# Two conv-sweep layers on one core: token scaling by a table of turns, uneven reciprocal groups, and norm stores from ScalarE's queue

## What is computed

```python
def sweep_fwd(seq, w):
    def step(carry, row):
        new = row + jax.nn.relu(conv1d(carry, w))
        return (new, new)
...
x = x + _L0_conv_ref(_ln_c(x), L0_conv_w_d, ...)      # norm 0, then the sweeps
t = t + _L0_ffn_ref(_ln_t(t), ...)                    # norm 1, then the experts
x = x + _L1_conv_ref(_ln_c(x), L1_conv_w_d, ...)      # norm 2, then the sweeps
t = t + _L1_ffn_ref(_ln_t(t), L1_ffn_W, ...)          # norm 3, batch statistics, then the recurrence
...
def step(yt, wx_t):
    yt = jax.nn.sigmoid(wx_t + yt @ Vt)
```

## Time and profile before

| what | value |
|---|---|
| time, median of 3 runs | 4235.26 us (4232.78 to 4238.69) |
| the profiled execution's own time | 4230.19 us |
| its span, first to last instruction | 4228.4 us |
| mean granted TensorE clock | 0.99 |
| TensorE matmuls busy | 4126.6 us (98%) |
| ScalarE busy | 2062.3 us (49%) |
| VectorE busy | 1328.9 us (31%) |
| norms 0, 1, 2, 3 in the chain that ended last | about 3 to 93, 948 to 1243, 1257 to 1371, 2228 to 2399 us |

### The profile page before, as it was taken

One profiled execution on the slowest core, in us unless ns is written; L12 is line 12 of the kernel. 1 busy time (PEld: TensorE's weight loads), 2 busy tenths in 40 slices (PEclk: granted clock), 3 DMA queues, 4 the chain that ended last, 5 costly groups with the idle time before them and its releaser, 6 DMA issues.

```text
span 4228.4 us, 138285 instructions
## 1 busy us (share of the span) xinstructions
PE 4126.6 (98%) x57200; PEld 3129.7 (74%) x57200; DVE 1328.9 (31%) x2576; ACT 2062.3 (49%) x8972; POOL 119.9 (3%) x243
## 2 busy tenths in 40 slices
PE   8999999998889999999998899999999999999999
PEld 3999999994442999999993466666666666666666
DVE  4655433334546655533335600000000000000000
ACT  6002344435545002344444366666666666666666
POOL 1000000000010000000000000000000000000000
PEclk9999999999999999999999899999999999999999
DMA  6000000004258000000007200000000000000000
GB/s 158 1 0 0 0 0 0 0 0 141 71 137 254 7 0 0 0 0 0 0 0 200 73 22 15 22 19 18 22 16 22 22 16 22 15 22 22 16 22 19
DMA packets 178469, 144.93 MB, mean 34 GB/s; under 512 B 110910, under 2 KB 177502, under 8 KB 178014
## 3 DMA queue, kind: packets, MB, share of 16 engines
q1 hardware_dynamic: 177486, 137.58, 12.4%
q10 hardware_dynamic: 528, 0.63, 0.1%
HBM read 79.19 MB, written 58.98 MB: 33 GB/s over the span
## 4 chain that ended last, share of the span: by engine, by line
PE 94%; DVE 2%; ACT 1%; issue 1%; SPq 1%; DMA 1%; POOL 0%; DVEq 0%; ACTq 0%; POOLq 0%
PE ps L977 24%; PE ps L827 22%; PE ps L798 18%; PE ps L896 16%; PE ps L891 3%; PE ps L600 2%; PE ps L635 1%; PE ps L594 1%; PE ps L611 1%; PE ps L768 1%; PE ps L621 1%; PE ps L868 1%; PE ps L666 1%; SPq L405 1%; PE ps L749 0%
## 5 line engine op out<-in xcount | busy, mean ns | idle before, releaser
L977 PE MATMUL ps<-xl,vt 65*32 65x8 f32 x28800 | 1693.3, 187 | 0.0
L1189 ACT ACTIVATE xl<-ps 64x8 f32<-64x8 f32 x7200 | 1224.0, 170 | 595.4 <-PE ps L977 1.5
L896 PE MATMUL ps<-idle 128*32 128x256 bf16 (+1 forms) x5828 | 1496.4, 271 | 3.6 <-POOL ident L514 3.6
L977 PEld LDWEIGHTS ps<-xl,vt 65*32 65x32 f32 x28800 | 1037.4, 108 | 622.1 <-ACT xl L1189 0.2
L827 PE MATMUL ps<-xl,taps 128*128 128x128 f32 (+2 forms) x7880 | 912.4, 279 | 4.7 <-DVE xl L1410 4.7
L827 PEld LDWEIGHTS ps<-xl,taps 128*128 128x128 f32 x7880 | 912.0, 191 | 5.4 <-issue 5.3
L798 PEld LDWEIGHTS ps<-split 128*128 128x128 f32 x4140 | 773.8, 189 | 10.7 <-issue 9.3
L798 PE MATMUL ps<-split 128*128 128x400 f32 x4140 | 780.6, 351 | 0.0
L1498 DVE TENSOR_TENSOR xl<-xl 64x320 f32<-64x320 f32 x180 | 125.2, 696 | 1695.2 <-ACT xl L1189 1695.2
L1044 ACT ACTIVATE img<-xl 128x144 f32 x788 | 366.8, 466 | 546.5 <-DVE xl L1400 546.5
L896 PEld LDWEIGHTS ps<-idle 128*32 128x32 bf16 x5828 | 577.5, 99 | 13.9 <-issue 3.6
(11 more groups left out here) (154 smaller groups left out, 1666.0 us busy)
## 6 DMA issues: line engine op xcount, KB each, us to landing
ring<-in_x_dram SPq DMA_DIRECT2D x144, 200.0 KB, 3.7
x_dram<-sums SPq DMA_DIRECT2D x144, 200.0 KB, 3.3
t_dram<-sums SPq DMA_DIRECT2D x72, 200.0 KB, 3.6
ring<-t_dram SPq DMA_DIRECT2D x72, 200.0 KB, 3.8
ring<-x_dram SPq DMA_DIRECT2D x72, 200.0 KB, 3.7
xl<-x_dram SPq DMA_DIRECT2D x45, 320.0 KB, 5.2
out_dram<-xl SPq DMA_DIRECT2D x45, 320.0 KB, 3.5
img<-in_L_ffn_weight_dram SPq DMA_DIRECT2D x4, 512.0 KB
```

The lines of the kernel that those rows point to most:

```text
L896: pe.matmul(PS[bank][0:32, 0:n], idle[:, 0:32], idle[:, 0:n], start=True, stop=True)
L977: last = pe.matmul(PS[2 * s + h][c * 32:(c + 1) * 32, t * HB:(t + 1) * HB], vt[:, c * 32:(c + 1) * 32], prev, start=False, stop=True, skip ...
L1189: act.activation(yb[0:64, s, h * HB:(h + 1) * HB, t], PS[2 * s + h][0:64, t * HB:(t + 1) * HB], ACT.Sigmoid).then_inc(step_y[h], 1)
```

## The change

- Groups have ends of their own (`GROUP_ENDS`): 10, 20, 30, 36 in norms 0 and 2 and 9, 18, 27, 36 in norm 1, as before; in norm 3 they are 10, 18, 26, 32 and 36, five groups instead of four.
- In norm 3 a table (`TOKEN_TURN`) says which units are spread and scaled in which turn: two in turn 13, one in 14 to 16, two in 17, one in 18 to 28, two in 29, 32, 35, 36, 37, 39 and 40, one in the others up to 34, none in 38. The loop has 41 turns on TensorE, 50 before. The seven banks are used from unit 28 (`TOKEN_TAIL`), not from 27.
- In norm 3 the reciprocals of a group are taken all four in turn end+2, right behind the sum and ahead of statistics and scaling. In norms 0 and 2 they stay in turns end+2 and end+3, two each, but stand ahead of the scaling. `low_taps` moves from turn 22 to 27.
- In norm 0 TensorE's pair of spreads in an odd turn stands behind `take_mean` and `variances`, not ahead.
- In norms 2 and 3 the two stores of a unit are issued by ScalarE, behind its copies of the unit and ahead of a root that is due. SyncE issues only the loads there.

```diff
-        GROUP = {0: NCH + 1, 1: NCH, 2: NCH + 1, 3: NCH}
+        GROUP_ENDS = {0: (10, 20, 30, UNITS), 1: (9, 18, 27, UNITS), 2: (10, 20, 30, UNITS), 3: (10, 18, 26, 32, UNITS)}
+        TOKEN_TURN = {n: list(range(a, b)) for n, a, b in zip(range(13, 42), (0, 2, 3, 4, 5, 7, 8, 9, *range(10, 18), 18, 20, 21, 22, 24, 25, 26, 28, 30, 32, 32, 34),
+                                                              (2, 3, 4, 5, 7, 8, 9, 10, *range(11, 19), 20, 21, 22, 24, 25, 26, 28, 30, 32, 32, 34, UNITS))}
+        TOKEN_TAIL = 28
...
+        def store(eng, i, n):
+            st = ln[i]
+            eng.wait_ge(st.summed, 2 * n + 2)
+            for h in range(2):
+                eng.dma_start(unit_tokens(DST[i], i, n, h), pair(half(unit_of(sums, n % RING), h))).then_inc(st.stored[n % RING], 16)
...
+                elif i == 1:
+                    store(sp, i, n)
                 else:
                     sp.wait_ge(st.summed, 2 * n + 2)
-                    for h in range(2):
-                        sp.dma_start(tokens(DST[i], n, h), pair(half(unit_of(sums, n % RING), h))).then_inc(st.stored[n % RING], 16)
...
+            def spread_out(n):
+                if n == TOKEN_TAIL:
+                    pe.wait_ge(st.kept, 2 * UNITS)
+                pe.wait_ge(st.inverse, INVERSES * (place_of(i, n)[0] + 1))
+                for v in range(2):
+                    j = 2 * n + v
+                    if j - 2 * TOKEN_TAIL >= len(TOKENS_LAST):
+                        pe.wait_ge(st.normed, j - len(TOKENS_LAST) + 1)
+                    elif j >= 2:
+                        pe.wait_ge(st.normed, min(j - 1, 2 * TOKEN_TAIL))
                     spread_one(pe, i, n, v, token_spread_bank(i, n, v))
...
-            for n in range(UNITS + LAG):
-                if LAG <= n:
-                    spread_out(n - LAG)
+            for n in range(max(TOKEN_TURN) + 1):
+                for m in TOKEN_TURN.get(n, []):
+                    spread_out(m)
                 if n + 1 < UNITS:
                     move(n + 1)
...
-                if LAG <= n < UNITS and (i == 2 or n % 2):
-                    for p in range(n - LAG - (i == 0), n - LAG + 1):
-                        spread_out(p)
+                if i == 2 and LAG <= n < UNITS:
+                    spread_out(n - LAG)
...
                     variances(pe, i, n - 1, row_squares)
+                if i == 0 and LAG <= n < UNITS and n % 2:
+                    for p in (n - LAG - 1, n - LAG):
+                        spread_out(p)
...
+                    if i == 2:
+                        store(act, i, n)
...
                     keep(n)
-                if n >= 2 and (n - 2) % NCH == NCH - 1:
-                    take_std(act, i, (n - 2) // NCH)
+                    store(act, i, n)
+                if n - 1 in GROUP_ENDS[i]:
+                    take_std(act, i, GROUP_ENDS[i].index(n - 1))
...
-            for n in range(UNITS + LAG + 1):
-                m = n - LAG - 1
+            scaled = []
+            for n in range(max(TOKEN_TURN) + 2):
                 if n < UNITS:
                     total(n)
-                if m >= 0:
+                if n - 2 in GROUP_ENDS[i]:
+                    for part in range(INVERSES):
+                        invert(dve, i, GROUP_ENDS[i].index(n - 2), part)
+                for m in scaled:
                     bn_take(dve, m, 0)
-                if LAG <= n < UNITS + LAG:
-                    scale(n - LAG)
-                if m >= 0:
+                for m in TOKEN_TURN.get(n, []):
+                    scale(m)
+                for m in scaled:
                     bn_take(dve, m, 1)
-                if NCH <= n < UNITS + NCH and 2 <= n % NCH < 4:
-                    for part in range(INVERSES // 2):
-                        invert(dve, i, n // NCH - 1, (n % NCH - 2) * INVERSES // 2 + part)
+                scaled = TOKEN_TURN.get(n, [])
...
+                for since in (3, 4):
+                    if n - since + 1 in GROUP_ENDS[i]:
+                        for part in range(INVERSES // 2):
+                            invert(dve, i, GROUP_ENDS[i].index(n - since + 1), (since - 3) * INVERSES // 2 + part)
                 if n >= LAG:
                     for h in range(2):
                         scale_row(dve, i, n - LAG, h)
...
-                elif n == LAG + 8:
+                elif n == LAG + 13:
                     low_taps(dve, i // 2)
```

More of the change, by code:

```diff
@@ L288, in metaformer @@
         INVERSES = 4
-        GROUP = {0: NCH + 1, 1: NCH, 2: NCH + 1, 3: NCH}
+        GROUP_ENDS = {0: (10, 20, 30, UNITS), 1: (9, 18, 27, UNITS), 2: (10, 20, 30, UNITS), 3: (10, 18, 26, 32, UNITS)}
+        TOKEN_TURN = {n: list(range(a, b)) for n, a, b in zip(range(13, 42), (0, 2, 3, 4, 5, 7, 8, 9, *range(10, 18), 18, 20, 21, 22, 24, 25, 26, 28, 30, 32, 32, 34),
+                                                              (2, 3, 4, 5, 7, 8, 9, 10, *range(11, 19), 20, 21, 22, 24, 25, 26, 28, 30, 32, 32, 34, UNITS))}
+        assert sum(TOKEN_TURN.values(), []) == list(range(UNITS))
+        TOKEN_TAIL = 28
         IN_NORM = UNITS - LAG
@@ L300, in place_of @@
         def place_of(i, n):
-            return n // GROUP[i], n % GROUP[i]
+            g = sum(n >= end for end in GROUP_ENDS[i])
+            return g, n - (GROUP_ENDS[i][g - 1] if g else 0)
         def group_end(i, g):
-            return min(GROUP[i] * (g + 1), UNITS)
+            return GROUP_ENDS[i][g]
         def row_spread_bank(i, p, h):
@@ L346, in token_spread_bank @@
                 return ROUTE_SPREAD[j % len(ROUTE_SPREAD)]
-            return SPREAD32[v] if n < LAST else TOKENS_LAST[(j - 2 * LAST) % len(TOKENS_LAST)]
+            return SPREAD32[v] if n < TOKEN_TAIL else TOKENS_LAST[(j - 2 * TOKEN_TAIL) % len(TOKENS_LAST)]
         def by_rows(t, hp):
@@ L393, in metaformer, with unit_tokens @@
         block = ctx.enter_context(nc.Block())
+        def unit_tokens(t, i, n, h):
+            g, k = group_of(i, n)
+            return t[h, :, 2 * g:2 * g + 2, k * CH:(k + 1) * CH]
+        def store(eng, i, n):
[3 more added lines that the diff above has]
+                eng.dma_start(unit_tokens(DST[i], i, n, h), pair(half(unit_of(sums, n % RING), h))).then_inc(st.stored[n % RING], 16)
         def sp_norm(sp, i, meanwhile=None):
             st = ln[i]
-            def tokens(t, n, h):
-                g, k = group_of(i, n)
-                return t[h, :, 2 * g:2 * g + 2, k * CH:(k + 1) * CH]
             def load(n):
                 for h in range(2):
-                    sp.dma_start(pair(half(unit_of(ring, n % RING), h)), tokens(SRC[i], n, h)).then_inc(st.loaded[n % RING], 16)
+                    sp.dma_start(pair(half(unit_of(ring, n % RING), h)), unit_tokens(SRC[i], i, n, h)).then_inc(st.loaded[n % RING], 16)
             for n in range(RING):
@@ L582, in variances @@
             st, (g, k) = ln[i], place_of(i, n)
-            size = group_end(i, g) - g * GROUP[i]
+            size = group_end(i, g) - (n - k)
             if k % 2 == 0 and k < size - 1:
@@ L637, in centre_and_project, with spread_routed @@
                 last.then_inc(st.centred, 1)
-            def spread_out(n):
+            def spread_routed(n):
                 g, k = n // NCH, n % NCH
-                banks = ROUTE_SPREAD if i == 1 else TOKENS_LAST if n >= LAST else SPREAD32
-                since = 2 * NCH * g if i == 1 else 2 * LAST if n >= LAST else 0
                 if k == 0:
-                    if i == 1 or n == LAST:
-                        pe.wait_ge(st.kept, 2 * (n + NCH))
-                    if i == 1:
-                        for _ in range(14):
-                            keep_clock(pe, 512, MOVE[1])
+                    pe.wait_ge(st.kept, 2 * (n + NCH))
+                    for _ in range(14):
+                        keep_clock(pe, 512, MOVE[1])
                     pe.wait_ge(st.inverse, INVERSES * (g + 1))
@@ L651, in spread_out @@
                     j = 2 * n + v
-                    if j - since >= len(banks):
-                        pe.wait_ge(st.normed, j - len(banks) + 1)
-                    elif j >= 2 and i == 3:
-                        pe.wait_ge(st.normed, min(j - 1, 2 * LAST))
+                    if j - 2 * NCH * g >= len(ROUTE_SPREAD):
+                        pe.wait_ge(st.normed, j - len(ROUTE_SPREAD) + 1)
+                    spread_one(pe, i, n, v, token_spread_bank(i, n, v))
+            def spread_out(n):
[8 more added lines that the diff above has]
+                        pe.wait_ge(st.normed, min(j - 1, 2 * TOKEN_TAIL))
                     spread_one(pe, i, n, v, token_spread_bank(i, n, v))
@@ L685, in pe_token_norm @@
                         if n < first + NCH:
-                            spread_out(n)
+                            spread_routed(n)
                         if n > first:
@@ L1308, in dve_row_norm @@
                         scale_row(dve, i, n - LAG, h)
-                for since in (3, 4):
-                    g = place_of(i, n - since)[0]
```

(5 more changed lines are left out.)

## The result

The changed kernel takes 4248.15 us (median of 6 runs, 4245.04 to 4253.32) beside 4233.23 us for the kernel before (6 runs, 4227.16 to 4238.69): a ratio of 1.0039, 95% interval 1.0028 to 1.0049. It is slower by 0.4%, near the 4250 us forecast. The profiled execution took 4247.86 us, its span is 4246.1 us, 17.7 more than before. The total is near by luck: it hides large errors of opposite sign, so the stages matter more than the sum.

The account below looks back on a forecast made before the run. TensorE, on the chain for 94% of the span, was taken as the bound. Norm 0 -6.8, norm 2 +4.8, norm 3 +13.9 and clock +3.5 gave +15.4 us, forecast 4250 us, range 4232 to 4264.

Parts of the forecast that it names:

- Norm 0: Norm 0: spreads behind the mean and reciprocals ahead of the scaling take 6.8 us off, 1.5 of it from the pairs.
- The reciprocals: Norm 0: reciprocals ready before the next group's first spread remove waits of 2.5 and 1.1 us and 1.7 of slow clock.
- The store on ScalarE: Norms 2 and 3: a unit's two stores occupy ScalarE's queue for 1.27 us, during which it starts nothing else.
- Turns 1 to 11: Start of norm 3: stores delay ScalarE's squares, a turn takes 3.66 us against 3.24, +4.6 us in all.
- a later group: Norm 3, groups ending at 18, 26, 32: reciprocals make a turn 3.5 us late, 2.25 without the store's 1.27; +10.5 in all.
- Rival 1: Norms 2 and 3: the issue costs ScalarE nearly nothing, overlapping running activations; 4233.5 us, up to 4240 with the clock; chance 0.18.
- Norm 2: Norm 2: later roots and scaling behind reciprocals cost +1.3, +1.5 and +2.0 us in three groups, +4.8 together.
- Where scaling starts: Norm 3: the first group of ten units, stores and undivided reciprocals make turn 14 begin later, +4.4 us.
- Double turns and late groups: Norm 3: second units and late reciprocals cost 3.3 + 10.5 + 3.7 us; a double turn costs 1.6 more.
- The clock: Norm 3: two of four new TensorE waits are followed by a fall of the clock, +3.5 us; bounds 0 and 15.
- Tail: End of norm 3: six units fewer are spread and scaled alone, 2.1 us each, -12.6 us.
- Rival 2: Norm 3: VectorE isn't late, reciprocals end before the next group's spread is due; faster, 4221 us; chance 0.12.

Follow-up runs that it names:

- stores_only: The kernel before with only the stores of norms 2 and 3 moved to ScalarE's queue: 4236.38 us, ratio 1.0010.
- norm0_order_only: The kernel before with only norm 0's order changed (reciprocals ahead of scaling, pairs of spreads behind the mean): 4221.61 us, ratio 0.9972.
- relaxed_late_second: relaxed_pairs with the second unit's spreads of a double turn moved behind the move of the next unit: 4228.11 us, ratio 0.9986.
- turns_only: The kernel before with only norm 3's table of turns, five groups and reciprocals in one piece, stores on SyncE: 4259.42 us, ratio 1.0067.
- relaxed_pairs: The kernel before with norm 0's new order and a norm 3 table asking for no group earlier than four turns after its end: 4236.67 us, ratio 1.0002.
- clock_fillers_free_bank: The changed kernel with idle matmuls in norm 3's waits, into a bank free after ScalarE's last copy: 4232.16 us, ratio 1.0000.
- relaxed_fillers: relaxed_pairs with three idle matmuls ahead of the second unit's spreads in each double turn: 4229.01 us, ratio 0.9991.

## Why the prediction was right, and where it wasn't

The total was right (+14.9 us by the medians, +15.4 forecast), and that was luck: norm 0 and the stores came out better than their terms, the clock worse, and the errors cancelled.

- **Norm 0.** -12.1 instead of -6.8 (the means above). "I take 0.15 to 0.3 us off ten pairs" is the step: it was read from TensorE's wait of 0.29, while the engine that set the pace was ScalarE, which lost 1.19 per pair. The reciprocals were right (5.5 against 5.3).
- **The store on ScalarE.** "During which ScalarE starts nothing else" was wrong; the price of 0.63 per transfer was right. Turns 1 to 11 lost next to nothing instead of 4.6, a later group 0.55 instead of 1.25. The first group lost 1.4, as forecast (1.3): turn 14 begins 49.3 us after the norm's start in stores_only and 48.0 in norm0_order_only. Rival 1's mechanism is the true one, and its 0.18 was too little. What it would have given for the total (4233.5) did not come, since the clock took more. The Trainium skill (DMA: Bandwidth & Descriptors, "Where the ~2 us actually goes") gives a dispatch some 50 ns, and the section is about transfers issued from GpSimd, which the prediction did not say; the rows of ScalarE's queue here show 0.60 to 0.65 us for each, and the cost is small because it is hidden.
- **Norm 2.** Predicted +4.8, measured +4.9 between the means of executions with either queue (+2.8 at a like clock). The mechanism was another: what separates the queues lies ahead of the first spread (+4.6), where sums wait for stores. The prediction had 3.5 of its 4.8 in the second and third group, behind it, where no difference shows. VectorE's three waits for a root did grow, from 3.2 us in all to 7.5. Why the stores land later for the sums is only argued: the store is issued behind ScalarE's copies, and SyncE's loads, no longer held by it, are queued sooner. No run separates the two.
- **Where scaling starts.** Turn 14 begins 52.3 us after the norm's start, 50.6 before: +1.7. But the execution before had the early spell; against norm0_order_only, which has neither that nor a change in norm 3, it is +4.4 (52.31 against 47.95), as forecast. The 4.6 of turns 1 to 11, which the prediction adds to it, did not come.
- **Double turns and late groups.** 17.5 predicted, at most 19.1 measured with the clock held up. The lateness was worked out nearly rightly: 2.9 for 3.5 in the second group, 2.3 for 2.25 without stores. A double turn costs 2.1, not 1.6.
- **The clock.** The mis-sized term of norm 3: "I count two of four: +3.5". It is at least 14.3 us, four spells, each of 7 to 14 us. The prediction priced a fall like the one in norm 0, where one pair was slow (1.7); here the spells are two to four times as long as the 3.4 us of that one. It looked for falls behind four waits, those for units 0, 10, 18 and 26. Two of them had one (units 18 and 26, in turns 29 and 35, which are double turns as well). The other two spells stand behind waits that it priced without a fall, those for the bank in turns 17 and 32, of 0.75 and 0.81 us. The wait of 1.79 us for unit 10 had none. The bound given for the clock, 15, held.
- **Tail.** -11.2 against -12.6.

Norm 3 against the execution before adds up as 4.4 + 19.1 + 14.3 - 11.2 - 2.6 = 24.0; the last term is the early spell that the kernel before had and the changed one did not.

Rival 2 (faster, VectorE not late) is refuted by more than this table: with hardly a late group (relaxed_late_second) norm 3 gained nothing.

## What to carry to other kernels

Before moving work forward, ask what it asks of the engine that is full there: a unit moved from a tail that VectorE fills into a loop that TensorE fills saved 1.8 to 1.9 us (9.1 for five, 11.2 for six) and cost 1.4 to 2.1, before any fall of the clock and any late group. Short waits on a TensorE that is nearly full are dear for what follows them, and idle matmuls into a free bank are a cheap way to find out how dear. Look for the pace-setting wait on every engine of a loop, not only on the one with the highest busy share; and time the parts of a bundled change apart, for here the one good part (norm 0's order, 0.9972) was hidden by a bad one (1.0067). And before two profiled executions are compared stage by stage, look at the clock of each stage in both.

## What the runs showed of the hardware

- A transfer on ScalarE's queue is issued while activations dispatched ahead of it still run: the first issue started with the last square (both at 2229.91).
- The granted clock fell to 0.50 behind a wait of TensorE of 0.75 us (turn 17 of the changed kernel), and not behind each of them: turn 17 of turns_only has the same wait and no fall. The Trainium skill (TensorE: Matmul & The Clock Gate, "A second HAM failure mode: psum-queue depth-cycling") tells of a kernel in which small idle times between groups of matmuls, as banks are cycled, let the gate swing to and fro; relaxed_pairs agrees in part: of its five double turns, three are followed by a spell at 0.50 (turns 16, 33 and 35, with waits of 0.75, 0.81 and 1.53 us) and two are not (turns 19 and 31, 0.75 us each). What decides between a fall and none stays open.
- Idle matmuls in such waits took falls away: the ratio went from 1.0039 to 1.0000 in the changed kernel (clock_fillers_free_bank) and norm 3 from 183.6 to 176.3 us in relaxed_pairs (relaxed_fillers).
